# Attention layer with a post-norm feed-forward: the last two heads and the first gate/up pair with their helper work in another order

## The chip, the core and the metric

The kernel runs on one core of a Trainium2 chip. The metric is the device time of the kernel in microseconds (us). Of the kernel before there are three runs: 1136.99, 1139.20 and 1139.71 us, with the median at 1139.2 us. One more execution, of 1139.85 us, was recorded by the profiler: its span from the first to the last instruction is 1138.0 us, and 1.85 us lie outside it. All rows below are from that execution, with times counted from the start of its span.

A core has five engines that run their own instruction queues in order and wait for each other by semaphores. PE (TensorE) multiplies matrices into PSUM. DVE (VectorE), ACT (ScalarE) and POOL (GpSimd) do the element-wise work. SP (SyncE) issues DMAs here, and ACT issues some too.

## The reference

The layer works on 1024 tokens of 512 features: causal attention with 32 heads of 128 and 8 key/value heads, a LayerNorm, a gated feed-forward of width 1792 behind an RMS norm, and a second LayerNorm. Cut to what is computed:

```python
q, k, v = x @ wq, x @ wk, x @ wv                 # 32, 8 and 8 heads of 128
q = q * cos + rotate_half(q) * sin               # k likewise; each k, v serves 4 heads
scores = where(tril, q @ k.T / sqrt(128), -inf)
att = softmax(scores)
x = layernorm(x + (att @ v) @ wo)
nx = x * rsqrt(mean(x * x) + 1e-5) * ln_w
x = layernorm(x + (silu(nx @ gate.T) * (nx @ up.T)) @ down.T)
```

Everything is float32 and must come out with nearly its accuracy.

## The kernel before, in words

**Products.** Each operand of a matmul is split in two: `hi` is the value rounded to the fast 32-bit format (written by ACT) and `lo = value - hi` (written by POOL or DVE). A product is then three matmuls, hi·hi, lo·hi and hi·lo (`product` in the tensor program, lines 1518 to 1520). A `lo` that comes late holds PE up.

**Heads.** The tokens are 8 row tiles of 128, in two halves of 4. For each head and each row tile, PE computes scores into `S`, DVE takes the row maximum (L1113), ACT the exponential (L769), DVE turns 32x32 blocks (L1126), and SP moves the turned pieces by DMA into `PT_lo` (L408). This is done in five sends per head (`SENT`, numbered k = 0 to 4: tiles 0-1, 2-3, 4-5, 6, 7). For each send ACT writes `PT_hi` (L776) and POOL or DVE the difference. Then PE multiplies with V ("pv", half 0 and half 1 of each head), ACT and DVE split the result into `O_hi` (L821) and `O_lo` (L1172), and PE multiplies it with `wo` (`rows(t)`, one of 8 per head). DVE adds each of these rows to `y` (L1187).

**The last two heads** (numbered 2 and 3 of their group) are interleaved by hand: 16 steps in the table `LATE`. Head 3 uses `xT_hi`/`xT_lo` as its `PT_hi`/`PT_lo`. Its two halves share one buffer, so the sends of half 1 may not start until PE is through with pv half 0. `late_high` (ACT) and `late_low` (POOL, L644) are the splits of these heads. Behind the table, PE runs pv half 1 of head 2, rows 4 to 7 of head 2, pv half 1 of head 3, and then goes over to the feed-forward.

**First LayerNorm and first gate/up pair.** The feed-forward is 7 pairs of 256 features. Pair 0 is computed plainly, the others by a scheme with block sums. For pair 0 DVE makes the RMS-normalised rows (`both_norm`, L1394, into `nx`), PE transposes them (L1634), and ACT and DVE split them (L854, L1408). `gate_up(0, u)` for u = 0 to 3 computes gate and up into a half of `S`: `bank` 0 is the gate, 1 is up, and u = 0, 1 are for token half 0, u = 2, 3 for half 1. For each u: ACT `silu` (L965), DVE `product` (L1295, gate times up), ACT `act_high` (L971, `K_hi`), POOL `act_low` (L672, `K_lo`). Then `down` multiplies with the down weights into `ACC`, one row tile t = 0 to 7 at a time, and DVE adds it to `y` (L1300). Tiles 4 to 7 need the `K_lo` of u = 2 and u = 3.

Between these, DVE normalises `y` itself in place (`layer_norm`, L1394, 8 rows). It also computes four differences of the transposed input (`x_diff`, L1304) that the block scheme needs, which ACT splits (`x_sum_high`, L994) and DVE or POOL completes (L1310, L694). POOL adds up the weights for pair 1 (`weight_sums`, L700 to L705), ACT splits them (L981), and DVE completes them (L1317). Then `blocks(1, 0)` runs on PE in seven groups of six matmuls, and DVE mixes the results (L1334 and on). PE may not start the sixth group until DVE's first mix has read its bank.

The order on every engine is simply the order of the code. `shift` (`-mean * inv_spread`) and the ACT form of the normalisation existed before for the output at the end of the kernel (`normalise`, L1088).

## Time and profile before

| What | Value |
|---|---|
| Median of three runs | 1139.2 us (1136.99 to 1139.71) |
| Profiled execution | 1139.85 us, its span 1138.0 us |
| PE busy over the span | 1100.1 us, 97% |
| DVE, ACT, POOL busy | 891.6, 643.2, 856.9 us |
| Mean granted TensorE clock | 0.994 of full speed |

A busy share is an average over the span. What matters for this change is the stretch between 860 and 960 us, in which the attention ends and the feed-forward begins. In a timeline row, the bracket at the end tells how long the engine had been idle before the instruction and whose work released it.

### The profile page before, as it was taken

The page shows a single profiled execution, that of the slowest core. Times are in us where ns is not written, and L with a number is a line of the kernel's source. Part 1 is how long each engine was busy: PE and PEld are TensorE (multiplying, and loading weights), DVE is VectorE, ACT ScalarE, POOL GpSimd, SP SyncE. Part 2 cuts the span into 40 slices and gives each one's busy share as a digit, 9 for nine tenths or more (in the row PEclk, how much of TensorE's full clock was granted, in tenths as well). Part 3 has the DMA queues.
Part 4 walks back from the last instruction along what each step waited for, and adds up shares of the span by engine and source line. Part 5 has one row for each costly group of instructions (what it writes and reads, how often), then busy time and mean ns, then how long its engine had stood idle before and what let it go on. Part 6 is the DMA issues. An engine that isn't in the chain of part 4 may idle for free.

```text
span 1138.0 us, 19115 instructions
## 1 busy us (share of the span) xinstructions
PE 1100.1 (97%) x5274; PEld 929.7 (82%) x5274; DVE 891.6 (78%) x1528; ACT 643.2 (57%) x1159; POOL 856.9 (75%) x584
## 2 busy tenths in 40 slices
PE   7899999999999999999999999999998798999997
PEld 6788888888888888888888888888776677888886
DVE  5788787778778787888787888788877798877767
ACT  4666566666666566656665666665655434333333
POOL 1699789978997898789789978997776647444431
PEclk9999999999999999999999999999999998999999
DMA  6856555555555565565555655555555401211101
GB/s 192 237 143 154 132 141 152 130 150 142 147 129 138 141 156 140 146 156 158 136 144 152 155 140 143 142 150 138 130 127 129 131 19 56 74 56 55 37 18 75
DMA packets 155550, 144.86 MB, mean 127 GB/s; under 512 B 15488, under 2 KB 135808, under 8 KB 155520
## 3 DMA queue, kind: packets, MB, share of 16 engines
q1 hardware_dynamic: 143360, 124.57, 42.2%
q10 hardware_dynamic: 12160, 19.93, 6.1%
q8 instruction: 14, 0.23, 0.1%
q14 instruction: 16, 0.13, 0.0%
HBM read 37.49 MB, written 2.10 MB: 35 GB/s over the span
## 4 chain that ended last, share of the span: by engine, by line
PE 37%; POOL 33%; issue 18%; DVE 4%; DMA 3%; ACT 2%; SPq 1%; ACTq 1%; POOLq 1%; DVEq 0%
POOL qk_raw L563 8%; PE ACC L1518 7%; POOL PT_lo L589 7%; PE ACC L1520 7%; PE ACC L1519 7%; POOL rope_s L564 6%; POOL Q_lo L573 4%; PE S L1518 4%; PE S L1519 4%; PE S L1520 4%; POOL wq_lo L542 2%; POOL wo_lo L542 2%; POOL qk_raw L567 1%; PE S L1534 1%; PE S L1536 1%
## 5 line engine op out<-in xcount | busy, mean ns | idle before, releaser
L1113 DVE CUSTOM_DVE_ANT_0 S<-S,mask 128x128 f32<-128x128 f32 (+7 forms) x256 | 194.2, 758 | 148.8 <-PE S L1536 148.7
L769 ACT ACTIVATE probs<-S,neg_max 128x128 f32<-128x128 f32 (+7 forms) x256 | 189.0, 738 | 191.8 <-DVE neg_max L1113 189.9
L589 POOL TENSOR_TENSOR PT_lo<-PT_lo,PT_hi 128x896 fp32r<-128x896 f32 (+1 forms) x90 | 191.6, 2129 | 21.5 <-ACT PT_hi L776 21.4
L1126 DVE STREAM_TRANSPOSE turned<-probs 128x128 f32<-128x128 f32 (+7 forms) x256 | 197.6, 772 | 2.5 <-ACT probs L769 2.5
L1187 DVE SCALAR_TENSOR_TENSOR y<-ACC,row_rcp,y 128x512 f32<-128x512 f32 x256 | 176.6, 728 | 4.4 <-PE ACC L1520 4.4
L563 POOL TENSOR_TENSOR qk_raw<-qk_raw,cos_sin 128x512 f32<-128x512 f32 x76 | 126.3, 1662 | 67.4 <-DMA rope_s<-qk_raw 67.0
L776 ACT ACTIVATE PT_hi<-PT_lo 128x896 fp32r<-128x896 f32 (+3 forms) x155 | 157.1, 1013 | 33.1 <-DMA PT_lo<-turned 32.8
L1534 PE MATMUL S<-K_hi,Q_hi 128*128 (+4 forms) x380 | 130.9, 344 | 4.4 <-ACT probs L769 4.4
L1518 PE MATMUL ACC<-PT_hi,V_hi 128*128 128x512 f32 x372 | 128.2, 345 | 5.0 <-POOL PT_lo L589 4.9
L1536 PE MATMUL S<-K_hi,Q_lo 128*128 (+4 forms) x380 | 129.4, 340 | 0.0
L1535 PE MATMUL S<-K_lo,Q_hi 128*128 (+4 forms) x380 | 129.3, 340 | 0.0
L1519 PE MATMUL ACC<-PT_lo,V_hi 128*128 128x512 f32 x372 | 129.2, 347 | 0.0
L1520 PE MATMUL ACC<-PT_hi,V_lo 128*128 128x512 f32 x372 | 128.9, 347 | 0.0
L567 POOL TENSOR_TENSOR qk_raw<-qk_raw,rope_s 128x512 f32<-128x512 f32 x76 | 117.7, 1548 | 6.0
L1133 DVE TENSOR_TENSOR PT_lo<-PT_lo,PT_hi 128x1536 fp32r<-128x1536 f32 (+1 forms) x60 | 113.8, 1897 | 1.8
L1518 PE MATMUL ACC<-wo_hi,O_hi 128*128 128x512 f32 x256 | 103.3, 404 | 8.0 <-DVE y L1187 4.4
L1518 PE MATMUL ACC<-xT_hi,wq_hi 128*128 128x512 f32 x256 | 101.9, 398 | 3.5 <-DVE xT_lo L1218 3.0
L1519 PE MATMUL ACC<-xT_lo,wq_hi 128*128 128x512 f32 x256 | 100.4, 392 | 0.0
L1520 PE MATMUL ACC<-xT_hi,wq_lo 128*128 128x512 f32 x256 | 100.4, 392 | 0.0
L1520 PE MATMUL ACC<-wo_hi,O_lo 128*128 128x512 f32 x256 | 100.0, 391 | 0.0
L1519 PE MATMUL ACC<-wo_lo,O_hi 128*128 128x512 f32 x256 | 99.8, 390 | 0.0
L564 POOL TENSOR_TENSOR rope_s<-rope_s,cos_sin 128x512 f32<-128x512 f32 x76 | 98.2, 1292 | 0.0
(260 smaller groups left out, 2567.8 us busy)
## 6 DMA issues: line engine op xcount, KB each, us to landing
PT_lo<-turned SPq DMA_DIRECT2D x248, 112.0 KB, 2.5
PT_lo<-turned SPq DMA_DIRECT2D x124, 208.0 KB, 4.0
rope_s<-qk_raw ACTq DMA_DIRECT2D x152, 128.0 KB, 3.6
PT_lo<-turned SPq DMA_DIRECT2D x124, 128.0 KB, 2.6
PT_lo<-turned SPq DMA_DIRECT2D x124, 80.0 KB, 2.3
wq_raw<-in_L_attn_wq_dram SPq DMA_DIRECT2D x32, 256.0 KB, 3.0
wo_raw<-in_L_attn_wo_dram SPq DMA_DIRECT2D x32, 256.0 KB, 3.9
V_stage<-in_L_ffn_down_w_t_dram SPq DMA_DIRECT2D x7, 512.0 KB, 3.5
```

Of the source, the lines that this page charges most:

```text
L563: nc.gpsimd.tensor_tensor(qk_raw[:, r], qk_raw[:, r], cos_sb[:, cols], ALU.mult).then_inc(product_done, 1)
L564: nc.gpsimd.tensor_tensor(rope_s[:, r], rope_s[:, r], sin_sb[:, cols], ALU.mult).then_inc(product_done, 1)
L589: nc.gpsimd.tensor_tensor(lo, lo.bitcast(F32), hi.bitcast(F32), ALU.subtract).then_inc(pt_lo_done[half], 1)
L769: nc.scalar.activation(dst, src, ACT.Exp, bias=neg_max[:, at:at + 1], scale=-1.0, accum_out=row_sum[:, j % 2, i:i + 1]).then_inc(exp_done, 1)
L776: nc.scalar.activation(of_tiles(pt[0], SENT[k]), of_tiles(pt[1], SENT[k]).bitcast(F32), ACT.Copy).then_inc(pt_hi_done[SENT[k][0] // HT], 1)
L1113: nc.vector.tensor_tensor_reduce(src, src, bias, scale=1.0, scalar=MASKED, op0=ALU.add, op1=ALU.min, accum_out=neg_max[:, at:at + 1]).then ...
L1126: nc.vector.transpose(dst.rearrange("p b (r i) -> p r b i", i=QB), src.rearrange("p (r b i) -> p r b i", b=4, i=QB)).then_inc(turn_done, 1)
L1187: nc.vector.scalar_tensor_tensor(out=y[:, t, :], in0=ACC[:, 1 + n.n["y"] % 2 * 2], scalar=row_rcp[:, head % 2, t:t + 1], in1=y[:, t, :], o ...
L1518: nc.tensor.matmul(dst, a[0], b[0], start=start, stop=False)
L1519: nc.tensor.matmul(dst, a[0], b[1], start=False, stop=False)
L1520: return nc.tensor.matmul(dst, a[1], b[0], start=False, stop=stop)
L1534: nc.tensor.matmul(dst, q[0], k[0], start=True, stop=False)
```

## The change

It touches one stretch of the program, from the third quarter of the `LATE` table to the first pair of the feed-forward:

1. In `LATE` step 7, ACT splits the pv result of head 2, half 0 (`O_hi`), ahead of the `PT_hi` of send 2 of that head instead of behind it.
2. The `lo` of the last send of head 3 (128 x 1024) goes from POOL to DVE, behind the add of rows 4 and 5 of head 2 and ahead of the norms of half 0. PE waits for a new semaphore `last_lo_done`.
3. `rows(4)` and `rows(5)` of the last head go ahead of the gate matmuls of `gate_up(0, 0)`, and `rows(6)` and `rows(7)` stay between gate and up.
4. The eight in-place normalisations of `y` are dealt out again. DVE keeps four (three behind `new_x_low(1)`, the fourth behind the third `x_diff`). ACT gets rows 4 to 7, three of them behind `silu(0, 2)` and one behind `act_high(0, 2)`. DVE computes `shift` for them in one small instruction, and its fifth `down_add` waits for ACT's four.
5. `product(0, 2)` goes ahead of `x_diff(2)` on DVE, and `act_high(0, 3)` ahead of `x_sum_high(4)` on ACT.

```diff
+        last_lo_done = sem("last_lo_done")
...
-            for k in (2, 3, 4):
+            for k in (2, 3):
                 late_low(k, REP - 1)
...
+                if s == 7:
+                    split_high("pv", 0)
                 if s in LATE_HIGH and s not in LATE_FIRST:
                     late_high(*LATE_HIGH[s])
...
-                    elif s != 13:
+                    elif s not in (7, 13):
                         split_high(kind, half)
...
             silu(0, 2)
+
+            def layer_norm(t):
+                nc.scalar.activation(y[:, t, :], y[:, t, :], ACT.Identity, bias=shift[:, t:t + 1],
+                                     scale=inv_spread[:, 0, t:t + 1]).then_inc(ln_done, 1)
+
+            act_e.wait_ge(shift_done, 1)
+            for t in range(HT, HT + 3):
+                layer_norm(t)
             act_high(0, 2)
+            layer_norm(NT - 1)
             x_sum_high(2, 3)
             silu(0, 3)
             x_sum_high(3, 3)
+            act_high(0, 3)
             x_sum_high(4, 4)
-            act_high(0, 3)
...
             add_rows(5, REP - 2)
+            dve.wait_ge(pt_hi_done[1], HEADS * 3)
+            hi, lo = [of_tiles(t, SENT[4]) for t in sources(REP - 1)]
+            nc.vector.tensor_tensor(lo, lo.bitcast(F32), hi.bitcast(F32), ALU.subtract).then_inc(last_lo_done, 1)
             inverses(0)
...
             product(0, 0, first=True)
+            half_1 = slice(HT, NT)
+            nc.vector.scalar_tensor_tensor(out=shift[:, half_1], in0=mean_var[:, half_1, 0], scalar=-1.0,
+                                           in1=inv_spread[:, 0, half_1], op0=ALU.mult, op1=ALU.mult).then_inc(shift_done, 1)
             new_x_low(1)
-            for t in tiles[0]:
-                layer_norm(t).then_inc(ln_done, 1)
+            for t in tiles[0][:3]:
+                layer_norm(t)
             product(0, 1, first=True)
-            for t in tiles[1]:
-                layer_norm(t).then_inc(ln_done, 1)
...
             x_diff(3, x_22, x_12)
+            product(0, 2, first=True)
             dve.wait_ge(x_sum_done, 2)
             x_diff(2, x_22, x_11)
-            product(0, 2, first=True)
+            layer_norm(HT - 1)
...
             blocks_low(1, 0)
+            dve.wait_ge(ln_done, HT)
             down_add(0, 4)
...
-                            pe.wait_ge(late_lo_done[late - 2], 3)
+                            pe.wait_ge(late_lo_done[late - 2], 3 if late == REP - 2 else 2)
+                            if late == REP - 1:
+                                pe.wait_ge(last_lo_done, 1)
...
-                        if first and (u, bank, c) == (0, 1, 0):
-                            for t in range(HT, NT):
+                        if first and u == 0 and c == 0:
+                            for t in (4, 5) if bank == 0 else (6, 7):
                                 rows(t)
```

On PE, at the passage from the transposes (`S<-ident,rope_s`) to the first gate matmuls (`S<-PT_hi,wq_hi`), this stood before:

```order
L1634 MATMUL S<-ident,rope_s 128x128 x3
L1518 MATMUL S<-PT_hi,wq_hi 128x512 [waits xt_lo_done,fw_lo_done]
L1519 MATMUL S<-PT_lo,wq_hi 128x512
L1520 MATMUL S<-PT_hi,wq_lo 128x512
L1518 MATMUL S<-PT_hi,wq_hi 128x512 [waits xt_lo_done]
```

And this stands there now (the changed kernel's line numbers are higher by 18 to 20 here):

```order
L1654 MATMUL S<-ident,rope_s 128x128 x3
L1536 MATMUL ACC<-wo_hi,O_hi 128x512 [waits wo_done,y_free,split_done,fw_lo_done]
L1537 MATMUL ACC<-wo_lo,O_hi 128x512
L1538 MATMUL ACC<-wo_hi,O_lo 128x512
L1536 MATMUL ACC<-wo_hi,O_hi 128x512 [waits y_free,wo_done]
L1537 MATMUL ACC<-wo_lo,O_hi 128x512
L1538 MATMUL ACC<-wo_hi,O_lo 128x512
L1536 MATMUL S<-PT_hi,wq_hi 128x512 [waits xt_lo_done]
```

Six matmuls of rows 4 and 5 now stand ahead of the first gate matmul, which used to be the first thing behind the transposes.

On DVE, between the split of the second half of the transposed input (`xT_lo<-ACC`) and the fourth product (`rope_s<-S,qk_raw`), this stood before (`x_diff` is the form with 128x1024, the norms are `y<-y,mean_var,inv_spread`):

```order
L1408 SCALAR_TENSOR_TENSOR xT_lo<-ACC,ln_w_sb,xT_hi 128x512 [waits xt_hi_done] x4
L1394 TENSOR_SCALAR y<-y,mean_var,inv_spread 128x512 x4
L1295 TENSOR_TENSOR rope_s<-S,qk_raw 128x512 [waits silu_done]
L1394 TENSOR_SCALAR y<-y,mean_var,inv_spread 128x512 x4
L1304 TENSOR_TENSOR turned<-probs,turned 128x1024 [waits x_right_done,x_left_done]
L1304 TENSOR_TENSOR probs<-turned,probs 128x1024 [waits x_right_done]
L1304 TENSOR_TENSOR turned<-turned 128x1024 [waits x_sum_done]
L1295 TENSOR_TENSOR rope_s<-S,qk_raw 128x512 [waits act_lo_done,silu_done]
L1304 TENSOR_TENSOR probs<-turned,probs 128x1024 [waits x_sum_done,x_left_done]
L1295 TENSOR_TENSOR rope_s<-S,qk_raw 128x512 [waits act_lo_done,silu_done]
```

And now:

```order
L1420 SCALAR_TENSOR_TENSOR xT_lo<-ACC,ln_w_sb,xT_hi 128x512 [waits xt_hi_done] x4
L1406 TENSOR_SCALAR y<-y,mean_var,inv_spread 128x512 x3
L1307 TENSOR_TENSOR rope_s<-S,qk_raw 128x512 [waits silu_done]
L1316 TENSOR_TENSOR turned<-probs,turned 128x1024 [waits x_right_done,x_left_done]
L1316 TENSOR_TENSOR probs<-turned,probs 128x1024 [waits x_right_done]
L1307 TENSOR_TENSOR rope_s<-S,qk_raw 128x512 [waits act_lo_done,silu_done]
L1316 TENSOR_TENSOR turned<-turned 128x1024 [waits x_sum_done]
L1406 TENSOR_SCALAR y<-y,mean_var,inv_spread 128x512
L1316 TENSOR_TENSOR probs<-turned,probs 128x1024 [waits x_sum_done,x_left_done]
L1307 TENSOR_TENSOR rope_s<-S,qk_raw 128x512 [waits act_lo_done,silu_done]
```

Ahead of the third product now stand three norms instead of eight and two `x_diff` instead of three. The fourth norm and the third `x_diff` come behind it.

On ACT, in the same stretch (`qk_raw<-S` is `silu`, `K_hi` is `act_high`, the 1024-wide ones are `x_sum_high`), this stands now:

```order
L968 ACTIVATE qk_raw<-S 128x512 [waits gu_done]
L1072 ACTIVATE y<-y,shift,inv_spread 128x512 [waits shift_done]
L1072 ACTIVATE y<-y,shift,inv_spread 128x512 x2
L974 ACTIVATE K_hi<-rope_s 128x512 [waits prod_done]
L1072 ACTIVATE y<-y,shift,inv_spread 128x512
L997 ACTIVATE xT_hi<-turned 128x2x512 [waits x_sum_done]
L968 ACTIVATE qk_raw<-S 128x512 [waits gu_done]
L997 ACTIVATE PT_hi<-probs 128x1024 [waits x_sum_done]
L974 ACTIVATE K_hi<-rope_s 128x512 [waits prod_done]
```

The four normalisations are new in it, and the last `K_hi` has moved ahead of one 1024-wide split.

## Rows read from the trace of the kernel before

**Rows 1.** Stretch, length, busy PE, PEld, DVE, ACT, POOL; granted clock, DMA share, GB/s.
```profile
898.00:902.00 4.00, 4.00 (x12) 3.09 (x11) 2.78 (x2) 0.00 (x0) 4.00 (x3) 0.57 0.00 0
944.00:949.00 5.00, 5.00 (x12) 3.93 (x13) 5.00 (x5) 1.14 (x2) 5.00 (x3) 0.50 0.00 0
960.00:1100.00 140.00, 140.00 (x618) 115.64 (x617) 104.51 (x146) 53.22 (x77) 65.53 (x61) 1.00 0.17 53
```
**Rows 2.** Timeline of PE: start, duration, instruction, idle before it and its releaser.
```profile
867.33 0.50 PE L1518 MATMUL ACC<-wo_hi,O_hi 128*128 128x512 f32 x1 [1.77 <-DVE O_lo L1172]
...
897.81 0.53 PE L1518 MATMUL ACC<-xT_hi,V_hi 128*128 128x512 f32 x1 [2.51 <-POOL xT_lo L644]
...
907.36 0.47 PE L1518 MATMUL S<-PT_hi,wq_hi 128*128 128x512 f32 x1 [1.33 <-DVE PT_lo L1408]
...
911.95 0.47 PE L1518 MATMUL ACC<-wo_hi,O_hi 128*128 128x512 f32 x1 [0.26 <-DVE y L1187]
...
918.88 1.47 PE L1634 MATMUL ACC<-ident,turned 128*128 128x128 f32 x12
...
929.21 0.50 PE L1518 MATMUL S<-xT_hi,wq_hi 128*128 128x512 f32 x1 [0.24 <-DVE rope_s L1295]
...
943.92 0.79 PE L1518 MATMUL ACC<-O_hi,K_hi 128*128 128x512 f32 x1 [3.54 <-POOL K_lo L672]
...
958.80 0.39 PE L1518 MATMUL S<-PT_hi 128*128 128x512 f32 x1
```
**Rows 3.** Timeline of POOL, the last head's splits and the first weights.
```profile
889.64 8.03 POOL L644 TENSOR_TENSOR xT_lo<-xT_lo,xT_hi 128x1536 fp32r<-128x1536 f32 x3 [4.61 <-ACT xT_hi L776]
900.46 2.56 POOL L678 TENSOR_TENSOR PT_lo<-cos_sin,PT_hi 128x1024 fp32r<-128x1024 f32 x1
```
**Rows 4.** Timeline of DVE, same stretch.
```profile
892.78 1.43 DVE L1187 SCALAR_TENSOR_TENSOR y<-ACC,row_rcp,y 128x512 f32<-128x512 f32 x2 [0.98 <-PE ACC L1520]
...
897.87 2.91 DVE L1394 TENSOR_SCALAR rope_s<-y,mean_var,inv_spread 128x512 f32<-128x512 f32 x2
```
**Rows 5.** DVE's split and norms: duration ns min/median/max; groups by form with mean ns.
```profile
L1394 DVE TENSOR_SCALAR y<-y,mean_var,inv_spread x9: 531/545/2620, 923.9 to 1134.4; 128x512 f32<-128x512 f32 x9
L1133 DVE TENSOR_TENSOR PT_lo<-PT_lo,PT_hi 128x1024 fp32r<-128x1024 f32 x30 | 48.9, 1631 | 1.8
```
**Rows 6.** Timelines of ACT and POOL around the DMAs of the last two heads.
```profile
865.03 1.28 POOL L563 TENSOR_TENSOR qk_raw<-qk_raw,cos_sin 128x512 f32<-128x512 f32 x1 [6.35 <-DMA rope_s<-qk_raw]
888.07 1.49 ACT L776 ACTIVATE xT_hi<-xT_lo 128x1536 fp32r<-128x1536 f32 x1 [1.39 <-DMA xT_lo<-turned]
892.44 1.06 ACT L776 ACTIVATE xT_hi<-xT_lo 128x1024 fp32r<-128x1024 f32 x1 [0.24 <-DMA xT_lo<-turned]
```
**Rows 7.** Timelines of DVE, ACT and POOL from the first product to the fourth.
```profile
923.86 4.69 DVE L1394 TENSOR_SCALAR y<-y,mean_var,inv_spread 128x512 f32<-128x512 f32 x4
929.07 3.30 DVE L1394 TENSOR_SCALAR y<-y,mean_var,inv_spread 128x512 f32<-128x512 f32 x4
940.14 0.69 DVE L1295 TENSOR_TENSOR rope_s<-S,qk_raw 128x512 f32<-128x512 f32 x1 [1.00 <-ACT qk_raw L965]
924.78 2.58 POOL L682 TENSOR_TENSOR O_lo<-V_stage,O_hi 128x1024 fp32r<-128x1024 f32 x1
942.59 1.27 POOL L672 TENSOR_TENSOR K_lo<-rope_s,K_hi 128x512 fp32r<-128x512 f32 x1 [2.29 <-ACT K_hi L971]
```
**Rows 8.** Timelines of ACT and DVE, the first mix; last row: ACT's normalisation at the end.
```profile
951.82 0.85 ACT L981 ACTIVATE PT_hi<-cos_sin 128x768 fp32r<-128x768 f32 x1 [6.68 <-POOL cos_sin L705]
957.77 0.68 DVE L1334 TENSOR_TENSOR qk_raw<-S,wq_raw 128x512 f32<-128x512 f32 x1
1126.29 0.80 ACT L1088 ACTIVATE y<-y,shift,inv_spread 128x512 f32<-128x512 f32 x1
```
**Rows 9.** The chain that ended last: a down matmul at each clock level.
```profile
944.71 0.43 PE ACC L1519
949.64 0.23 PE ACC L1519
```

More of the change, by code:

```diff
@@ L1086, in normalise @@
             def normalise(t):
-                act_e.wait_ge(shift_done, t + 1)
+                act_e.wait_ge(shift_done, t + 2)
                 nc.scalar.activation(y[:, t, :], y[:, t, :], ACT.Identity, bias=shift[:, t:t + 1],
```

## The prediction

> **What bounds the kernel now.** I read the busy times by stretch first. From 960 to 1100 us PE works in all 140 of 140 us at full clock [rows 1], so nothing done elsewhere shortens that part. PE must be gained between 860 and 960 us. There the timeline of PE shows six pauses that this change touches, 1.77, 2.51, 1.33, 0.26, 0.24 and 3.54 us long, the last of them ahead of down tile 4 [rows 2]. Behind the 2.51 us and the 3.54 us pause PE also ran for a while at the lower of its two clock levels, 1.2 instead of 2.4 GHz: the granted clock is 0.57 from 898 to 902 us and 0.50 from 944 to 949 us, with 12 matmuls in each [rows 1]. A matmul takes 0.43 us there and 0.23 us at the full level [rows 9]. So a pause costs its length and then up to 12 x 0.20 = 2.4 us more. Behind the 1.77 us pause the matmul on the same tile form took 0.50 us, the usual first one, and no stretch of low clock followed.
>
> Next I read the timelines of the helpers at these pauses. The 2.51 us pause ends on POOL, which does the three splits of the last head in a row, 8.03 us [rows 3]. The 3.54 us pause ends on `K_lo` of the fourth product, started at 942.59 us, and behind that stands DVE: its fourth product is at 940.14, after eight norms (4.69 + 3.30 us) and four differences [rows 7].
>
> **One fact of the rows decides the durations on DVE.** A norm of 128x512 takes 0.545 us in the median and 2.62 us at worst [rows 5]. The worst lies in the group of four that starts at 923.86 and takes 4.69 us, and in it POOL has a 1024-wide split of 2.58 us that starts at 924.78 [rows 7]. The two norms from 897.87 on, with POOL busy until 903.02, took 2.91 us together [rows 3, 4]. So a norm beside a busy POOL lasts until POOL's instruction is through. DVE's 1024-wide split takes 1.63 us in the mean [rows 5]. The Trainium skill (page SBUF — State Buffer, section Who interferes with whom) says that DVE with two inputs in SBUF, or in a two-port mode, and GpSimd take their shared ports for a whole instruction, whichever starts first, and the other blocks. By that rule the split moved to DVE would wait out POOL's and then run at its undisturbed time; by the mean alone it would end some 0.6 us sooner, and the sum would be 9.1 instead of 8.5.
>
> **Part 1, `O_hi` ahead of `PT_hi` in step 7.** ACT no longer holds `O_hi` back until a send has landed, so the 1.77 us pause goes. What is late next is POOL: its rope work starts only when a DMA lands at 865.03 [rows 6], and everything up to the pv of head 3 half 0 hangs on POOL's queue behind it. I see no way past that, so PE gives the 1.77 us back within 12 us. What can remain is that the send of head 3 half 1 (landed before 888.07) lands up to 1.4 us sooner, the time that ACT waited for it [rows 6]. DVE binds there after part 2, so I take 0, with bounds 0 and 1.4 gained.
>
> **Part 2, the last split on DVE.** POOL's three splits end at 897.67 (889.64 + 8.03). The third, 1024 wide, is about 2.4 us of it, so POOL is through at 895.3. DVE finishes rows 4 and 5 at 894.21 (892.78 + 1.43) [rows 4], and its input is ready since 893.50 (892.44 + 1.06) [rows 6]. It waits out POOL until 895.3 and takes 1.1: 896.4. PE starts pv at 896.5 instead of 897.81, 1.3 sooner. The pause is then 1.2 us, less than those without a low clock behind them, so I take the full clock and pv ends at 901.4 instead of 904.1. Queued behind the moved split on DVE are four norms and two row adds (1.4). The first norm waits out `wq_lo`, delayed itself, until 897.7 and ends at 898.2; adds to 899.6; the second norm waits out the 1024-wide weight split of 2.56 us [rows 3] until 901.7 and ends at 902.2; the other two meet an idle POOL: 903.2. That is 2.4 later than before (900.78), and PE's transposes wait for it. The transposes end at 903.8, the first gate operand is ready at about 905.0, where it was 907.36 [rows 2].
>
> **Part 3, rows 4 and 5 ahead of the gate.** `O_lo` stands behind the last norm on DVE: 903.9. Six matmuls of 0.23 us follow, 903.9 to 905.3. They fill the pause in which PE waited for DVE (1.33 us before), so the gate starts at 905.3: **2.1 us** gained so far. Later there are six matmuls less, 1.4 us, and the wait of 0.26 for a free bank goes with its 0.1 us of restart: **1.8 us**. The transposes of half 1 start at 915.0 instead of 918.88 (3.9). Their rows are ready: DVE's adds, statistics and norms of half 1 take 8.0 us from the first add (911.06 to 919.08 before) and start at 906.9, so they end at 914.9. That is a near tie; if it is missed, by tenths.
>
> **Parts 4 and 5, DVE's and ACT's queue up to the fourth product.** Call the start of these transposes T = 915.0. DVE's `xT_lo` ends at T+5.0 as before, 920.0. The three norms end with POOL's two instructions (K_lo and the 2.58 us one, up to about 923.4) and 0.5 after: 923.9. The product of u = 1 ends at 924.6, and gate_up(0, 3) may start at 925.1 without a wait: **0.3** (0.24 and its restart). Then two differences, 1.1 and, waiting out POOL, 2.3: 928.2. Third product 928.8, third difference 930.4, fourth norm 931.2, fourth difference 932.9, fourth product 933.5. ACT in the meantime needs 4 x 0.80 = 3.2 us at most for its normalisations [rows 8], three of them 925.8 to 928.1, while it would wait for the third product anyway, and the fourth behind `K_hi`: nobody waits. Before, ACT could do `silu` and `K_hi` at the same places. `K_hi` of u = 3 is done at 934.2, `K_lo` at 935.5. PE is through with gate_up(0, 3) at 930.5 and with down tiles 0 to 3 at 936.0. So the 3.54 us pause and its low clock go: 3.54 + 2.4 = **5.9**. The margin is half a microsecond.
>
> **What is late next.** From the start of the fourth `K_lo` (942.59) to the end of DVE's first mix (957.77 + 0.68 = 958.45) [rows 7, 8] it is 15.9 us: POOL's V_lo, its weight sums (for which ACT waits 6.68 us [rows 8]), ACT's and DVE's splits and two adds. None of it changes. With `K_lo` at 934.2 the mix ends at 950.1. PE needs it for the sixth block group, which was at 958.80 [rows 2], 0.35 us behind the mix; it would come there at 958.80 - 10.1 = 948.6 now. So a new pause of **1.5 us** opens. Bounds: 0, if weight sums and splits meet less of each other, and 3.
>
> **The sum.** 2.1 + 1.8 + 0.3 + 5.9 - 1.5 = 8.6 us. The profiled execution took 1139.85 us, so this gives 1131.3. It was 0.65 above the median of the three runs; taking half of that off I predict **1131.0 us**. The small additions (`shift`, 0.15 us; the wait of the fifth down add, for a normalisation finished 10 us before) stand beside waits.
>
> **Rivals.**
> - *B: the pause ahead of down tile 4 survives in part.* My margin there is 0.5 us, and four instructions on DVE each hang on how POOL's fall. If `K_lo` comes 2 us later, PE pauses 1.5 us and may fall to the low clock. But the chain to the first mix binds anyway and then ends 2 us later, 952.1: the sum is 6.3, and the time 1133.4. For it: 0.5 us is less than one blocked norm. Against: the working above already counts most of these instructions as blocked.
> - *C: the pause ahead of down 4 stays whole, with its low clock.* Then only 2.1 + 1.8 and the 0.3 remain, 4.2 minus the half of 0.65: 1135.4. For it: five of DVE's norms gone from before the third product are at least 5 x 0.545 = 2.7 us, less than the 5.9 to be removed, if POOL's work shifts so that none of the blocked time goes. Against: 4.69 + 3.30 us for eight shows that half was blocked time.
> - *D: the change gives nothing that can be measured.* The pause in front of the sixth group grows to 7 us, because POOL's weight sums are themselves blocked by a DVE queue that no longer idles: about 1138. For it: these sums are what ACT waits longest for. Against: before, DVE had only 1.0 us idle in that stretch too.
> - *E: slower.* DVE now stands still until the last send of head 3 has landed and ACT has split it, and behind this wait are two row adds, four norms and PE's pv. Before, POOL waited for it alone. Each microsecond that this send is late is then paid in full. It takes 8.6 us of lateness to eat the gain and 12 to be 3.4 us slower (1143). ACT waited 0.24 us for it before [rows 6], and no pause for a send in these rows is longer than the 6.35 us of the rope, so this is unlikely.
>
> **How the numbers follow.** Forecast A (1128.6 to 1133) has 58%, B 19%, C 10%, D 6%, E 3%. The remaining 4% is a gain larger than 10.5 us, with both bounds of part 1 and of the new pause in its favour. What a measurement of this kernel can tell from no change is 0.3%, 3.4 us: faster means under 1135.8. A, B, the rest and two thirds of C are faster, 88%; the rest of C and most of D are the same, 8%; E and a little of D are slower, 4%. The range from 1127.8 to 1135.8 leaves out D and E, some of C and of the large gains. For A alone it is 1128.6 to 1133.
>
> **What would show it.** Right: PE's pv of the last head starts near 896.5 with no low clock behind it; rows 4 and 5 lie between transposes and gate, which starts near 905.3; the transposes of half 1 are near 915; no pause ahead of down tile 4, which starts near 936; a pause of 1 to 2 us ahead of the sixth block group, released by DVE's first mix near 950; the rest as before, moved by 8.6. Wrong: a low clock at any of these places, a fourth product later than 934.5, or a moved split on DVE that ends after 897.

## The result, and the profile after

The changed kernel took 1129.48 us in the median of four runs (1127.02 to 1129.65). The kernel before took 1139.21 us beside it (1136.99 to 1139.71, four runs). The two medians lie 9.7 us apart, a quotient of 0.9915. The comparison on record gives a ratio of 0.993, 95% interval 0.9917 to 0.9944: 8.0 us faster (6.4 to 9.5). With four runs on either side the two figures differ, and I go by the smaller gain. Predicted were 1131.0 us and 8.2 us less than the median before. In a later comparison on another occasion it took 1128.37 us against 1136.66 us, ratio 0.9928 (0.9914 to 0.9943), and there the medians, 8.3 us apart, say the same. The profiled execution took 1129.51 us, its span 1127.7 us (before 1139.85 and 1138.0).

The span is 10.3 us shorter, which is more than the ratio says. The timeline of ACT shows why. Its copy of the last head's queries (`qk_raw<-ACC`) stands ahead of everything that the change moves. It started at 858.15 us before and now at 856.31, and in the other changed kernels below anywhere from 854.5 to 857.5. Nothing that the change moves stands ahead of it, so I do not count these two microseconds to the change. Below I measure from landmarks on PE inside the changed stretch: *pv0* and *pv1* are the starts of pv half 0 and half 1 of the last head, then come the first gate matmul, *T* (the first transpose of half 1, at 918.88 us before and 911.75 now), down tile 4, and the sixth block group.

| PE's stretch, us | before | after | after, second profile | change predicted |
|---|---|---|---|---|
| pv0 to the gate | 29.47 | 26.73 | 26.31 | -2.1 |
| gate to T | 11.52 | 9.67 | 9.69 | -1.8 |
| T to down tile 4 | 25.04 | 22.72 | 22.74 | -3.8 |
| down tile 4 to the sixth group | 14.88 | 13.75 | 13.61 | -0.9 |
| sixth group to the end | 179.20 | 179.48 | 179.47 | 0 |
| sum | 260.11 | 252.35 | 251.82 | -8.6 |

From the gate on, every stretch repeats within 0.15 us between the two profiles, which the whole time does not. Ahead of the gate they differ by 0.4 us, because the first profile has a stretch of low clock around pv0 (last section). This is the timeline of PE of the changed kernel at the places of [rows 2]:

```profile
875.35 0.77 PE L1536 MATMUL ACC<-xT_hi,V_hi 128*128 128x512 f32 x1 [0.50 <-POOL xT_lo L645]
...
894.12 0.47 PE L1536 MATMUL ACC<-xT_hi,V_hi 128*128 128x512 f32 x1 [1.20 <-DVE xT_lo L1442]
...
900.62 0.47 PE L1536 MATMUL ACC<-wo_hi,O_hi 128*128 128x512 f32 x1
...
902.08 0.46 PE L1536 MATMUL S<-PT_hi,wq_hi 128*128 128x512 f32 x1
...
911.75 1.48 PE L1654 MATMUL ACC<-ident,turned 128*128 128x128 f32 x12
...
934.47 0.50 PE L1536 MATMUL ACC<-O_hi,K_hi 128*128 128x512 f32 x1 [1.67 <-POOL K_lo L673]
...
948.22 0.50 PE L1536 MATMUL S<-PT_hi 128*128 128x512 f32 x1 [1.19 <-DVE qk_raw L1346]
```

The first line is pv0 and the 128x128 one is T. The 2.51 us pause is 1.20 us, rows 4 and 5 fill the pause ahead of the gate, the 3.54 us pause is 1.67 us, and a new one of 1.19 us has opened ahead of the sixth group. The stretches by window show the clock (columns as in [rows 1]; the granted clock is the third number from the end):

```profile
896.00:900.00 4.00, 4.00 (x28) 3.63 (x28) 3.02 (x6) 0.60 (x1) 1.65 (x1) 1.00 0.00 0
934.00:939.00 5.00, 4.53 (x20) 3.74 (x21) 5.00 (x4) 0.07 (x1) 5.00 (x3) 1.00 0.01 3
948.00:953.00 5.00, 4.79 (x20) 3.79 (x21) 3.93 (x7) 2.65 (x5) 3.15 (x5) 1.00 0.62 194
960.00:1100.00 140.00, 140.00 (x618) 115.64 (x618) 100.40 (x141) 50.46 (x73) 62.60 (x57) 1.00 0.15 45
```

The granted clock is 1.00 where it was 0.57 and 0.50. From 960 us on PE is as full as before. The helpers around pv1, POOL and DVE, beside [rows 3, 4]:

```profile
886.03 5.61 POOL L645 TENSOR_TENSOR xT_lo<-xT_lo,xT_hi 128x1536 fp32r<-128x1536 f32 x2 [3.12 <-ACT xT_hi L777]
891.59 1.30 POOL L679 TENSOR_TENSOR wq_lo<-turned,wq_hi 128x512 fp32r<-128x512 f32 x1
```
```profile
891.73 2.24 DVE L1442 TENSOR_TENSOR xT_lo<-xT_lo,xT_hi 128x1024 fp32r<-128x1024 f32 x1
```

The moved split became ready just as POOL began `wq_lo`. It took 2.24 us, where 1.63 was the mean of this form [rows 5], and released PE. And from the third product to the first mix, DVE, POOL and ACT, beside [rows 7, 8]:

```profile
924.86 0.68 DVE L1307 TENSOR_TENSOR rope_s<-S,qk_raw 128x512 f32<-128x512 f32 x1
...
929.15 0.68 DVE L1307 TENSOR_TENSOR rope_s<-S,qk_raw 128x512 f32<-128x512 f32 x1
929.75 1.21 DVE L1322 TENSOR_TENSOR xT_lo<-turned,xT_hi 128x1024 fp32r<-128x1024 f32 x1
930.88 1.27 DVE L1312 TENSOR_TENSOR y<-ACC,y 128x512 f32<-128x512 f32 x2
932.08 1.21 DVE L1322 TENSOR_TENSOR PT_lo<-probs,PT_hi 128x1024 fp32r<-128x1024 f32 x1
...
947.49 0.67 DVE L1346 TENSOR_TENSOR qk_raw<-S,wq_raw 128x512 f32<-128x512 f32 x1
```
```profile
928.22 1.61 POOL L706 TENSOR_TENSOR turned<-turned 128x256 f32<-128x256 f32 x1
929.79 4.63 POOL L673 TENSOR_TENSOR K_lo<-rope_s,K_hi 128x512 fp32r<-128x512 f32 x2
934.39 3.24 POOL L695 TENSOR_TENSOR V_lo<-probs,V_hi 128x1024 fp32r<-128x1024 f32 x1
```
```profile
922.61 2.22 ACT L1072 ACTIVATE y<-y,shift,inv_spread 128x512 f32<-128x512 f32 x3
925.57 0.64 ACT L974 ACTIVATE K_hi<-rope_s 128x512 fp32r<-128x512 f32 x1 [0.75 <-DVE rope_s L1307]
926.11 0.80 ACT L1072 ACTIVATE y<-y,shift,inv_spread 128x512 f32<-128x512 f32 x1
...
941.54 0.85 ACT L984 ACTIVATE PT_hi<-cos_sin 128x768 fp32r<-128x768 f32 x1 [7.47 <-POOL cos_sin L706]
```

ACT's four normalisations take 0.74 to 0.80 us each and stand where ACT would wait. The fourth product starts at T + 17.4 and ends at T + 18.1, where the prediction had its end at T + 18.5. Yet both last `K_lo` start only at 929.79, behind POOL's weight sums, and take 4.63 us instead of 2.6. DVE is never idle beside them: a 1024-wide split, two down adds, another 1024-wide split, two more down adds.

### The profile page after: what moved, and what is told of

It is laid out like the page before. It is cut to its first block, busy times and chain, and to the rows that moved or that the text cites. A ratio compares the mean times of both kernels' runs of the same rounds, so it can differ in the third digit from the quotient of the medians.

```text
span 1127.7 us, 19116 instructions
## 1 busy us (share of the span) xinstructions
PE 1097.1 (97%) x5274; PEld 928.8 (82%) x5274; DVE 887.9 (79%) x1526; ACT 646.5 (57%) x1163; POOL 856.7 (76%) x583
## 4 chain that ended last, share of the span: by engine, by line
POOL 37%; PE 37%; issue 17%; DVE 3%; DMA 3%; ACT 2%; POOLq 1%; ACTq 1%; SPq 1%; DVEq 0%
POOL qk_raw L564 8%; POOL PT_lo L590 8%; PE ACC L1536 8%; PE ACC L1538 7%; PE ACC L1537 7%; POOL rope_s L565 6%; POOL Q_lo L574 4%; PE S L1536 3%; PE S L1537 3%; PE S L1538 3%; POOL wq_lo L543 2%; POOL wo_lo L543 2%; POOL qk_raw L568 2%; PE S L1552 1%; DMA rope_s<-qk_raw 1%
## 5 line engine op out<-in xcount | busy, mean ns | idle before, releaser
L590 POOL TENSOR_TENSOR PT_lo<-PT_lo,PT_hi 128x896 fp32r<-128x896 f32 (+1 forms) x90 | 196.0, 2178 | 22.9 <-ACT PT_hi L777 22.5
L568 POOL TENSOR_TENSOR qk_raw<-qk_raw,rope_s 128x512 f32<-128x512 f32 x76 | 112.8, 1484 | 6.0
```

The costliest lines, as they stand in the source:

```text
L590: nc.gpsimd.tensor_tensor(lo, lo.bitcast(F32), hi.bitcast(F32), ALU.subtract).then_inc(pt_lo_done[half], 1)
```

## The experiments

All start from the changed kernel. They were run on three occasions, on which the kernel before took 1138.16, 1137.13 and 1136.66 us in the median (1139.21 with the result above), so whole times of different occasions compare only by their ratios to it. The whole times have intervals of 1.4 to 2.3 us to either side, so most verdicts rest on the stretches of the profiles, one profile of each kernel. "pv1", "T to down 4" and so on are starts on PE as above; "mix" is the start of DVE's first mix, L1346 in the changed kernel. Six profiles of kernels that differ only ahead of T agree behind it: down tile 4 at T + 22.72 to 22.75, mix at T + 35.62 to 35.74, sixth group at T + 36.35 to 36.47, the end 179.46 to 179.56 behind it.

**Part 2 back, part 1 back, both back.** The first gives POOL its third split again; the second takes this out of ACT's step 7; the third does both.

```diff
-            for k in (2, 3):
+            for k in (2, 3, 4):
                 late_low(k, REP - 1)
...
-            dve.wait_ge(pt_hi_done[1], HEADS * 3)
-            hi, lo = [of_tiles(t, SENT[4]) for t in sources(REP - 1)]
-            nc.vector.tensor_tensor(lo, lo.bitcast(F32), hi.bitcast(F32), ALU.subtract).then_inc(last_lo_done, 1)
```
```diff
-                if s == 7:
-                    split_high("pv", 0)
```

Part 2 back. 

> The changed kernel with the last 1024-wide split back on POOL. The step of my prediction says that the move lets pv of the last head start 1.2 us sooner: undone, pv starts 1.2 us later and the kernel takes 1 to 2.5 us longer, about 1131 us. Rival theory after the trace of the changed kernel: DVE's split there waited out two of POOL's instructions and ended at 893.97 us, where POOL alone would end near 894.05 (886.03 + 5.61 + 2.4), so the move itself gains nothing at pv: pv starts within 0.3 us of where it does now, counted from pv of head 3 half 0, DVE's norms are done 1 to 2 us sooner, and the time is within 0.5 us of the changed kernel's, about 1129.5 us.

Measured: 1129.12 us (1128.54 to 1131.41), ratio to before 0.9929 (0.9912 to 0.9945). The rival held: pv1 is 18.33 us behind pv0 (18.77 and 18.37 with all parts), its pause is 1.20 us, released by POOL now, and the clock holds. With part 1 in place, the move of the split gains nothing.

```profile
893.42 0.47 PE L1533 MATMUL ACC<-xT_hi,V_hi 128*128 128x512 f32 x1 [1.20 <-POOL xT_lo L645]
```

Part 1 back. 

> Part 1 alone taken back; the last split stays on DVE. Theory: the moved split always waits out the POOL instruction that runs when it becomes ready and the one behind it, so it ends where POOL's third split would have ended, and the gain of 1.1 us with the clock that holds comes from part 1 alone: pv of the last head 19.8 to 20.0 us behind pv of half 0 (18.8 with all parts), a pause of 2.3 to 2.5 us with the low clock behind it, the kernel at 1131 to 1132 us. Rival (the prediction's step for part 2): the split waits out only the POOL instruction that it meets: pv at 18.8, pause 1.3 us, no low clock, 1129.5 us.

Measured: 1130.31 us, 0.9951 (0.9935 to 0.9966). The theory fell and the rival held: the pause at pv1 is 1.10 us and the clock holds. ACT splits the first send of half 1 later here (886.55 us, 10.6 us behind pv0 instead of 9.1), the last one not (14.8 us behind pv0 instead of 14.9), and DVE ends at 894.74, in time. On the same occasion the changed kernel took 1128.37 us, 0.9928 (0.9914 to 0.9943); the intervals overlap.

```profile
894.89 0.48 PE L1534 MATMUL ACC<-xT_hi,V_hi 128*128 128x512 f32 x1 [1.10 <-DVE xT_lo L1440]
```

Both back. 

> Parts 1 and 2 both taken back, the rest stays. Theory: moving the split to DVE gains nothing because POOL would be through at the same time, and what made POOL's three splits of the last head earlier is part 1 (O_hi ahead of PT_hi on ACT), which lets the last sends come 1.1 us sooner. Then with both back, pv of the last head starts about 19.9 us behind the pv of half 0 (18.8 in the changed kernel, 18.3 with only part 2 back), its pause is 2.3 to 2.5 us and the clock drops behind it (1.5 us more); the kernel takes 1131 to 1132.5 us. Rival: neither part reaches the end, the 1.1 us is chance of the single executions: the pause stays at 1.2 us, no low clock, 1129.5 us.

Measured: 1130.63 us, 0.9945 (0.9924 to 0.9965). The whole time can't tell it from the changed kernel, and the profiled execution (1133.48 us) was the slowest of five. But the theory holds in the stretch: pv1 is 20.05 us behind pv0. PE's timeline of this kernel has the old pause, and its matmuls behind it take 0.63 us:

```profile
896.58 0.69 PE L1531 MATMUL ACC<-xT_hi,V_hi 128*128 128x512 f32 x1 [2.51 <-POOL xT_lo L645]
897.07 0.63 PE L1532 MATMUL ACC<-xT_lo,V_hi 128*128 128x512 f32 x1
```

PE's stretch from pv1 to the first transposes of the last head is 6.30 us, as before the change (6.29), and 4.75 in every other kernel: the low clock costs 1.55 us. So the pause at pv1 has two cures, either of which is enough: with both parts it is 1.20, with one 1.20 or 1.10, with none 2.51. From pv0 to the gate it takes 26.3 us with both (in the profiles with no low clock around pv0), 26.3 with part 1 alone, 27.1 with part 2 alone and 29.6 with neither. Part 1 has something of its own besides. In the kernel without it alone, the old pause ahead of head 2's rows stood again, with a low clock behind it:

```profile
864.48 0.50 PE L1534 MATMUL ACC<-wo_hi,O_hi 128*128 128x512 f32 x1 [1.82 <-DVE O_lo L1182]
864.82 0.46 PE L1535 MATMUL ACC<-wo_lo,O_hi 128*128 128x512 f32 x1
865.08 0.63 PE L1536 MATMUL ACC<-wo_hi,O_lo 128*128 128x512 f32 x1
```

From ACT's copy of the queries to pv0 this one took 20.7 us, the kernels with part 1 took 18.7 to 20.2. The other kernel without part 1 had a pause of 1.02 us there, no low clock and 19.0 us, and the kernel before 19.7. Whether part 1 gains anything ahead of pv0 stays open.

**Part 3 back:** rows 4 to 7 together between gate and up.

```diff
-                        if first and u == 0 and c == 0:
-                            for t in (4, 5) if bank == 0 else (6, 7):
+                        if first and (u, bank, c) == (0, 1, 0):
+                            for t in range(HT, NT):
                                 rows(t)
```

> The changed kernel with all four rows of the last head between gate and up again. My theory, that rows 4 and 5 fill time in which PE waits for DVE anyway: the gate starts at the same place, within 0.2 us, and the transposes of half 1 come 1.4 to 1.8 us later, as does everything behind them: about 1131.1 us. Rival, that the two pauses further on take up the difference, since they wait for DVE and POOL: the transposes come later, but a pause shrinks by as much, and the time stays within 0.4 us of the changed kernel's, 1129.5 us.

Measured: 1131.05 us (1129.58 to 1132.04), 0.9935 (0.9919 to 0.9952). From pv1 to the gate it takes 8.0 us as with all parts. The pause of 1.33 us ahead of the gate and the one of 0.26 us behind it are back. From the gate to T it takes 11.53 us instead of 9.67, and from pv1 to T 1.9 us more. Behind T nothing differs (down tile 4 at T + 22.73, sixth group at T + 36.36, end at T + 215.82), so the 1.9 us reach the end. The theory holds.

**Part 4 back, part 5 back, both back.** Part 4: three norms behind the first product and four behind the second, all on DVE, the eighth where it was. Part 5: the third product behind `x_diff(2)`, the last `K_hi` behind `x_sum_high(4)`. Both: DVE's and ACT's order of the kernel before.

```diff
             product(0, 1, first=True)
+            for t in tiles[1]:
+                layer_norm(t)
...
-            act_e.wait_ge(shift_done, 1)
-            for t in range(HT, HT + 3):
-                layer_norm(t)
             act_high(0, 2)
-            layer_norm(NT - 1)
```
```diff
-            product(0, 2, first=True)
             dve.wait_ge(x_sum_done, 2)
             x_diff(2, x_22, x_11)
+            product(0, 2, first=True)
...
-            act_high(0, 3)
             x_sum_high(4, 4)
+            act_high(0, 3)
```

Part 4 back. 

> The changed kernel with its eight normalisations dealt out as before: DVE does rows 4 to 7 too, behind its second product, and ACT none (the shift instruction goes as well). My theory, that the queue of DVE up to the fourth product sets the pause ahead of down tile 4: the fourth product comes 2.5 to 3.3 us later, the pause grows from 1.67 us to 4 to 5 us with a stretch of low clock behind it (2.4 us), and the kernel takes 4 to 6 us longer than the changed one, about 1134.5 us. Rival, that the gain behind the transposes comes from the earlier gate alone and ACT's help is worth nothing: within 1 us of the changed kernel, about 1129.5 to 1130.5 us.

Part 5 back. 

> Part 5 taken back: product(0, 2) behind x_diff(2) on DVE, act_high(0, 3) behind x_sum_high(4) on ACT. Theory: K_hi of u = 3 is 1.05 us later, so K_lo is, and the pause ahead of down tile 4 grows from 1.67 to about 2.7 us, the whole to 1130.5 us; no more, since everything to the first mix moves with it. Rival: POOL is held up by DVE until the same moment (its two K_lo took 4.63 us where two alone take 2.6), so the later K_hi is hidden: pause 1.67, 1129.5 us.

Both back. 

> Parts 4 and 5 taken back together: eight norms on DVE, four behind the first product and four behind the second, and the old order of the third product and of the fourth K_hi; parts 1 to 3 stay. Theory: PE's stretch from the transposes of half 1 to down tile 4 is then that of the kernel before, 25.0 us (22.7 with all parts), with a pause of about 3.5 us and the low clock behind it (2.4 us); the pause ahead of the sixth group is gone, because down tile 4 and all behind it is late, and the kernel takes 1132 to 1133 us. Rival: parts 1 to 3 have moved POOL's and DVE's meeting points, the pause stays under 3 us and the clock holds, as with part 4 alone taken back (2.59 us): 23.6 us, 1131 us.

| Kernel | median us, ratio (95%) | T to down 4, pause | mix at T + | T to sixth group, pause | end behind it |
|---|---|---|---|---|---|
| all parts | 1129.48, 0.993 (0.9917 to 0.9944) | 22.72, 1.67 | 35.74 | 36.47, 1.19 | 179.5 |
| part 5 back | 1129.70, 0.9936 (0.9917 to 0.9954) | 22.08, 1.05 | 35.97 | 36.70, 2.08 | 181.0 |
| part 4 back | 1132.33, 0.9948 (0.9931 to 0.9965) | 23.64, 2.59 | 37.63 | 38.36, 2.19 | 181.0 |
| both back | 1133.35, 0.9972 (0.9959 to 0.9984) | 25.07, 3.50 | 38.91 | 39.64, 0.45 | 179.5 |
| before | | 25.04, 3.54 | 38.89 | 39.92, 0 | 179.2 |

With both back the 3.50 us pause and the low clock are there again, and parts 4 and 5 together are worth 3.2 us from T to the end (219.10 against 215.95; before 219.12). The theory holds there. The whole times show 5.0 us: on the same occasion the changed kernel took 1128.37 us, and the intervals of the ratios, 0.9914 to 0.9943 and 0.9959 to 0.9984, lie apart. What goes beyond the 3.2 us stands in the profiles ahead of T (at 911.50 us against 909.78), where the two programs do the same, and I can't explain it. PE's timeline and the window behind it:

```profile
936.57 0.50 PE L1529 MATMUL ACC<-O_hi,K_hi 128*128 128x512 f32 x1 [3.50 <-POOL K_lo L673]
```
```profile
936.00:941.00 5.00, 4.43 (x12) 3.50 (x13) 5.00 (x5) 1.79 (x3) 5.00 (x3) 0.66 0.00 0
```

The sixth group has a pause of 0.45 us in this kernel, where my expectation had none. With part 4 alone back, the fourth product came 3.2 us later, as expected, but the pause ahead of down tile 4 was 2.59 us and not 4 to 5: POOL's `K_lo` no longer stood behind the weight sums, and the last was done at 935.04. The row names DVE's first down adds, which ended in the same moment. The expected low clock came not there but behind the sixth group's pause, which had grown:

```profile
935.09 0.50 PE L1530 MATMUL ACC<-O_hi,K_hi 128*128 128x512 f32 x1 [2.59 <-DVE y L1308]
...
949.81 0.50 PE L1530 MATMUL S<-PT_hi 128*128 128x512 f32 x1 [2.19 <-DVE qk_raw L1342]
```
```profile
950.00:954.00 4.00, 4.00 (x12) 3.14 (x12) 3.04 (x5) 1.86 (x3) 1.96 (x4) 0.62 0.67 211
```

So part 4 is worth 3.4 us from T to the end (219.35 against 215.95): 1.9 in the mix and 1.5 in the clock behind it. With part 5 alone back, both expectations had the place wrong. The pause ahead of down tile 4 became shorter, 1.05 us, not longer: POOL's last `K_lo` stood beside DVE's down adds and took 1.27 us. But the mix did not come sooner, so the sixth group waited longer and the clock fell there. Part 5 is worth 1.8 us from T to the end in the profiles (217.71 against 215.95), nearly all of it the clock, which the whole times (ratios 0.9936 and 0.993) can neither show nor exclude.

The two parts do not add up. From T to the end it takes 219.10 us with neither part in the kernel, 219.35 with only part 5 in it, 217.71 with only part 4 and 215.95 with both: part 5 gains nothing until part 4 is there.

**The four first down adds ahead of the two 1024-wide splits on DVE.**

```diff
-            x_sum_low(2, 1)
             down_add(0, 0)
             down_add(0, 1)
-            x_sum_low(3, 2)
+            x_sum_low(2, 1)
             down_add(0, 2)
             down_add(0, 3)
+            x_sum_low(3, 2)
```

> The changed kernel with DVE's down adds of tiles 0 and 1 ahead of its first 1024-wide completion of the differences, and those of tiles 2 and 3 ahead of the second. Theory, that in the changed kernel DVE's 1024-wide instruction with two inputs in SBUF (929.75 to 930.96, and the one at 932.08) holds POOL's two K_lo up, which took 4.63 us together where two take 2.6 alone, while adds that read PSUM do not: the two K_lo take 2.6 to 3.2 us together, the pause of 1.67 us ahead of down tile 4 goes, the pause ahead of the sixth block group grows from 1.19 us to between 1.2 and 2.9, and the kernel is 0 to 1.7 us faster than the changed one. Rival, that POOL's K_lo are slow from the weight sums ahead of them or from something that is not DVE: they still take over 4 us and nothing changes, 1129.5 us.

Measured: 1131.35 us (1129.15 to 1133.13), 0.9936 (0.9919 to 0.9953). POOL's two `K_lo` take 3.53 instead of 4.63 us, and the pause ahead of down tile 4 is 0.58 us. So DVE's order does hold POOL up, as the theory said, though 3.53 us is more than its 2.6 to 3.2, and the kernel is not 0 to 1.7 us faster. PE's timeline and the window show that more was lost than gained:


```profile
935.72 0.50 PE L1536 MATMUL ACC<-O_hi,K_hi 128*128 128x512 f32 x1 [0.58 <-POOL K_lo L673]
...
950.34 0.50 PE L1536 MATMUL S<-PT_hi 128*128 128x512 f32 x1 [2.04 <-DVE qk_raw L1346]
```
```profile
950.00:955.00 5.00, 4.66 (x13) 3.72 (x14) 3.51 (x7) 1.86 (x3) 3.12 (x5) 0.66 0.63 201
```

The mix is at T + 35.52, as it was. What down tile 4 gained the sixth group waited, and the end is at T + 217.2 instead of 215.9.

**The first mixes ahead of the last two down adds, alone and with the down adds first.**

```diff
-            down_add(0, 6)
-            down_add(0, 7)
             mixes(1, 0, first=True)
+            down_add(0, 6)
+            down_add(0, 7)
```

Alone. 

> In the changed kernel, the two down adds of tiles 6 and 7 go behind the first mixes on DVE. Theory: the pause of 1.19 us ahead of the sixth block group waits for DVE's first mix, and in front of it stand those two adds (1.28 us), which nothing waits for. Without them the pause goes: 1.2 us less, 1128.3 us. Rival: the adds stand beside other waits of DVE (for PE's banks), or the mixes then meet POOL's weight sums, and the pause comes back at the seventh group or the next pair: 1129.5 us.

Measured: 1128.44 us (1127.45 to 1131.50), 0.993 (0.991 to 0.995). The mix is at T + 34.57, the pause ahead of the sixth group is gone, and the sixth group stands at T + 35.31. Behind it 0.4 us is given back (179.86), so 0.8 us of the expected 1.2 is left.

With the down adds first. 

> The four first down adds ahead of the two 1024-wide lows on DVE (as in the earlier experiment, where the pause ahead of down tile 4 fell from 1.67 to 0.58 us while the one ahead of the sixth group grew from 1.19 to 2.04 us, with a stretch of low clock of 1.5 us behind it), and the first mixes ahead of the last two down adds. Theory: the second pause falls to 0.8 us and the clock holds, so both gains add up: 1.1 + 0.4 = 1.5 us less than the changed kernel, 1128.0 us. Rival: the mix is bound by the weight sums' chain and not by the adds in front of it; then the pause stays at 2.0 us with its low clock: 1130.9 us.

Measured: 1127.45 us (1125.76 to 1128.81), 0.9918 (0.9899 to 0.9937). The theory holds in the stretches. Both pauses are short and the clock holds; the end is at T + 214.23, 1.7 us sooner:

```profile
931.42 0.50 PE L1536 MATMUL ACC<-O_hi,K_hi 128*128 128x512 f32 x1 [0.55 <-POOL K_lo L673]
...
944.28 0.50 PE L1536 MATMUL S<-PT_hi 128*128 128x512 f32 x1 [0.29 <-DVE qk_raw L1346]
```

**The changed kernel and this version side by side.**

The changed kernel. 

> The changed kernel once more, for a comparison with the next kernel on the same chip: 1129.5 us, and where its landmarks lie in a second execution: pauses of 1.7 and 1.1 us ahead of down tile 4 and of the sixth group, no low clock in this stretch. What differs from its first execution is the chance of single executions.

The version with both edits. 

> The changed kernel with the four first down adds ahead of the two 1024-wide lows and the first mixes ahead of the last two down adds, beside the changed kernel. Theory: 1.5 to 2 us less than it, as the stretches of its first profile say (end of the program 227.1 us behind the first transposes of the last head against 228.8). Rival: the difference of the first medians (1127.45 to 1129.5) was chance: under 0.5 us.

Measured: 1128.37 us (1126.76 to 1129.66) for the changed kernel, 1129.96 us (1128.21 to 1132.53) for the other; ratios to before 0.9928 (0.9914 to 0.9943) and 0.9942 (0.9926 to 0.9958). In the stretch it was built for, the version is ahead again (end at T + 214.69 against 215.82). But its profiled execution had a low clock behind pv0 that the changed kernel's had not, 1.5 us. Over both occasions the version stands at 0.9918 and 0.9942, the changed kernel at 0.993 and 0.9928. On this occasion it was 1.6 us slower, which neither theory nor rival had. I can't show that it is faster as a whole.

## Why the prediction was right, step by step

The time and the range held, and so did the mechanism in the main: helpers kept PE waiting, and taking work out of their queues shortened the waits and the low clock behind them. Two steps were off, the credit for the stretch ahead of the gate and the pause ahead of down tile 4. By its own steps:

- **Part 1** was taken as 0 with bounds 0 and 1.4. The first send of half 1 did come sooner: ACT's 1536-wide `xT_hi` starts 9.1 us behind pv0, where it was 10.2 before (and 10.3 and 10.6 in the two kernels without part 1). The last send did not (14.9, before 14.6). But POOL's row of splits begins with the first one, and so ends sooner. With part 2 in place this changes nothing in the pause at pv1, as predicted (1.10 without part 1, 1.20 with it), and gains 0.8 us up to the gate, within the bounds. What the step did not see is that part 1 is enough without part 2.
- **Part 2**: pv1 1.3 us sooner, pause 1.2, full clock. Measured 1.2 to 1.6 us sooner, counted from pv0, pause 1.2 and full clock. But the credit is wrong: beside part 1 the moved split gains nothing, and without part 1 it gains 1.1 us (pv1 at 18.98 instead of 20.05 us behind pv0). The detail was off too. The split did not wait out the end of POOL's second split but met the weight split behind it, which had begun 0.14 us before, and took 2.24 us. Of the predicted delay of DVE's norms, 2.4 us, only 0.6 came (0.2 in the second profile), counted from pv0, since POOL's weight splits had moved up too. So pv0 to the gate gained 2.7 to 3.2 us instead of **2.1**.
- **Part 3**: **1.8** us predicted; 1.85 us measured between gate and T, and 1.9 when taken back.
- **The 0.3 us** ahead of gate_up(0, 3): the pause of 0.24 us is gone; with parts 4 and 5 taken back it returns with 0.26.
- **Parts 4 and 5, 5.9 us, is the step that was mis-sized.** It said that the 3.54 us pause and its low clock go, with a margin of 0.5 us, and its sign, no pause ahead of down tile 4, failed. The low clock went: without it and without a pause the stretch from down tile 4 to the sixth group takes 12.56 us (the kernel with the mixes first), before it took 14.88, so it cost 2.3 (predicted 2.4; in the kernel with parts 4 and 5 back it cost 1.6). But 1.67 us of the pause stayed, and the gain is 4.2 us. PE was ready at T + 21.05, as worked out (T + 21.0). `K_lo` was done at T + 22.7 instead of T + 20.5, although the fourth product was early. I had counted how POOL's instructions block DVE's, four times over, and not once how DVE's block POOL's. The weight sums (0.73 us where undisturbed, 0.92 to 1.77 here) pushed the third `K_lo` behind the fourth product, and both then ran beside DVE's 1024-wide instructions. This is rival B's mechanism, a lateness of 2 us for which I had written 1.5 us of pause.
- **The new pause, -1.5**: 1.19 and 1.07 us. From the start of `V_lo` to the end of the first mix it took 13.8 us, before 14.6.

Against the terms, the stretch ahead of the gate gave 0.6 to 1.1 us more, the one up to down tile 4 gave 1.5 less, the next 0.2 to 0.4 more, and 0.3 was lost behind. That they nearly cancel is luck in the stretch ahead of the gate. In the others it is not luck alone: the chain to the first mix binds. The mix stays at T + 35.5 to 36.0 whether down tile 4 starts at T + 21.6, 22.1 or 22.7. It ended at T + 36.4, where the forecast had 35.1 and B 37.1. So B named the right pause and charged too much for it: `K_lo` came 2.2 us later than forecast, but the mix 1.3 us and not 2.

Rival C's pause is that of the kernel with parts 4 and 5 back. D's 7 us pause and E's late send did not come: DVE's split found its input ready (ACT's `xT_hi` ended at 891.28, the split began at 891.73).

Three figures of the prediction are slips that move nothing: its "8.5" for the sum is the 8.6 of the sum itself; B's sum, 2 us less than that, is 6.6 and not 6.3, so 1133.0 us; and in the stretch that D speaks of, DVE before was idle for another 1.83 us (at 952.70) beside the 1.0.

## What to carry to other kernels

When PE waits twice behind the same chain of helpers, find the instruction that ends the chain and work on it. Making the first wait shorter only made the second longer (0.58 and 2.04 instead of 1.67 and 1.19 us), and the longer one dropped the clock. Of two engines that block each other on the same memory, count the blocked time on both. And where the whole time scatters by 2 us, stretches between landmarks in a profile resolve a tenth: part 3's 1.9 us was plain there, while the intervals of the whole times overlap.

## What the runs showed of the hardware that I had not expected

- **The length of a pause does not alone decide whether the clock falls.** Ahead of down tile 4 pauses of 0.55 to 2.59 us left it at 1.00 and those of 3.50 and 3.54 us did not. Ahead of the sixth group 2.04, 2.08 and 2.19 us dropped it each time, and 1.19 or less never. Around pv0 the same pair of pauses (1.22 to 1.27 us, then 1.52 to 1.59) left it alone in six profiles and dropped it in three. Behind the first pause at that place, 1.39 us, it fell in the changed kernel's first profile, and behind 1.41 and 1.42 us it held in four others, the kernel before among them. What decides besides the length, these runs do not show. A fall costs 1.5 us behind pv0, pv1 and the sixth group, and behind the pauses of 3.50 and 3.54 us 1.6 and 2.3. The fall behind 1.39 us, in PE's timeline:

```profile
872.51 0.47 PE L1552 MATMUL S<-K_hi,Q_hi 128*128 128x448 f32 x1 [1.39 <-ACT probs L770]
...
873.15 0.57 PE L1554 MATMUL S<-K_hi,Q_lo 128*128 128x448 f32 x1
873.52 0.57 PE L1552 MATMUL S<-K_hi,Q_hi 128*128 128x448 f32 x1
```

- **DVE and POOL block each other in both directions.** Two `K_lo` on POOL took 2.6 us when undisturbed and 4.63 us beside DVE's two 1024-wide splits; a norm of 0.54 us on DVE took up to 2.6. The Trainium skill (page SBUF — State Buffer, section Who interferes with whom) says that either holds the shared ports for a whole instruction. The traces agree: the `K_lo` begun at 929.79, beside DVE's split that ended at 930.96, took 2.33 us, 1.2 of them behind that end. So a handful of instructions on both engines can settle in more than one pattern: `wo_lo<-cos_sin` on DVE took 1.21 us in one execution of the last version and 1.75 us in the other, and the mix came 0.55 us later.
